# A fused convolution and mixture-of-experts kernel: TensorE multiplies the identity before its first tile, and the first tile's Toeplitz columns come in three parts instead of two

## The reference

```python
x = x + tanh(g_xattn[0]) * xattn(ctx, ctx, layernorm(x), ssm_kernel, D, 8)
x = x + tanh(g_ffn[0]) * ffn(layernorm(x), gate_w, w1, w2, w3, sw1, sw2, sw3)
```

## Time and profile before

| | |
|---|---|
| median of 3 runs | 742.96 us |
| lowest, highest | 740.34, 745.32 us |
| profiled execution, span | 739.8 us |
| TensorE, VectorE, ScalarE, GpSimd busy | 717.1, 568.5, 459.4, 363.4 us |
| TensorE in the first 11.3 us | 0.65 us busy |
| TensorE, 14.5 to 17.4 us | 2.85 us busy |

### The profile page before, as it was taken

How to read it: one execution, slowest core, us unless ns; L and a number is a source line. 1 busy time by engine, 2 the same in 40 slices (tenths; PEclk the granted TensorE clock), 3 DMA queues, 4 the chain that set the end, 5 groups by cost and what they waited for, 6 DMA issues and landing times.

```text
span 739.8 us, 15553 instructions
## 1 busy us (share of the span) xinstructions
PE 717.1 (97%) x4602; PEld 676.3 (91%) x4602; DVE 568.5 (77%) x1111; ACT 459.4 (62%) x659; POOL 363.4 (49%) x190
## 2 busy tenths in 40 slices
PE   3999999999999999999999999999999999999998
PEld 3999999999998999899989999988989999999997
DVE  7899999999965578428899588848987699679942
ACT  6575757575432222126878588847885789578931
POOL 4999888887401065042435433543634354434320
PEclk9999999999999999999999999999999999999999
DMA  6678687877522122463667577766565764432101
GB/s 231 215 239 288 218 272 216 279 218 253 186 85 60 29 43 29 144 197 90 161 201 218 131 232 210 198 176 168 145 182 160 176 193 90 74 68 46 30 1 57
DMA packets 48404, 114.88 MB, mean 155 GB/s; under 512 B 7472, under 2 KB 8624, under 8 KB 48336
## 3 DMA queue, kind: packets, MB, share of 16 engines
q1 hardware_dynamic: 35792, 89.67, 37.1%
q0 software_dynamic: 12544, 24.40, 17.9%
HBM read 157.78 MB, written 29.26 MB: 253 GB/s over the span
## 4 chain that ended last, share of the span: by engine, by line
PE 69%; DVE 13%; DMA 6%; issue 5%; ACT 3%; SPq 1%; ACTq 1%; POOL 1%; DVEq 1%; POOLq 0%
PE pair L1303 19%; PE bank L1303 15%; PE pair L1328 12%; PE pair L1234 8%; PE bank L1328 6%; PE bank L1185 4%; PE pair L1311 3%; DMA out<-ys,slot_info 3%; DMA raw<-in_weights 2%; PE bank L1245 2%; DVE prod L829 2%; DVE bank L834 2%; DVE x L800 2%; DVE w_lo L1150 1%; DVE rows L841 1%
## 5 line engine op out<-in xcount | busy, mean ns | idle before, releaser
L1150 DVE TENSOR_TENSOR w_lo<-raw,w_hi 128x1408 fp32r<-128x1408 f32 x94 | 148.5, 1621 | 47.0 <-ACT w_hi L733 47.0
L1441 POOL DMA_INDIRECT out<-ys,slot_info x47 | 80.6, 1714 | 120.6 <-ACT ys L721 87.3
L1428 POOL DMA_INDIRECT tn<-t_rows,slot_info x47 | 75.5, 1605 | 123.1 <-DVE tT_lo L888 90.6
L733 ACT ACTIVATE w_hi<-raw 128x1408 fp32r x94 | 124.6, 1374 | 2.1 <-issue 1.4
L1234 PE MATMUL pair<-kv_hi,toep_hi 128*128 128x288 f32 x320 | 100.6, 314 | 1.7 <-DMA toep_lo<-kpad_lo 1.4
L1234 PE MATMUL pair<-kv_lo,toep_hi 128*128 128x288 f32 x320 | 95.3, 298 | 0.0
L1234 PE MATMUL pair<-kv_hi,toep_lo 128*128 128x288 f32 x320 | 95.1, 297 | 0.0
L1155 DVE TENSOR_TENSOR w_lo<-raw,w_hi 128x1536 fp32r<-128x1536 f32 x47 | 82.3, 1752 | 4.5 <-ACT w_hi L740 4.5
L1379 POOL TENSOR_TENSOR kv_lo<-kv,kv_hi 128x2304 fp32r<-128x2304 f32 x15 | 77.3, 5153 | 5.9 <-ACT kv_hi L625 5.9
L740 ACT ACTIVATE w_hi<-raw 128x1536 fp32r x47 | 69.3, 1474 | 0.1
L829 DVE TENSOR_TENSOR prod<-pair,q 128x256 f32<-128x256 f32 x128 | 53.4, 417 | 15.1 <-PE pair L1234 9.6
(11 more groups left out here) (223 smaller groups left out, 2009.3 us busy)
## 6 DMA issues: line engine op xcount, KB each, us to landing
raw<-in_weights SPq DMA_DIRECT2D x94, 704.0 KB
raw<-in_weights SPq DMA_DIRECT2D x47, 768.0 KB
toep_hi<-kpad_hi SPq DMA_DIRECT2D x15, 512.0 KB, 4.6
toep_lo<-kpad_lo SPq DMA_DIRECT2D x15, 512.0 KB, 6.2
cx<-in_ctx SPq DMA_DIRECT2D x15, 384.0 KB, 6.3
stage<-in_weights SPq DMA_DIRECT2D x16, 272.0 KB, 6.7
xt<-in_x SPq DMA_DIRECT2D x16, 256.0 KB, 6.4
xr<-in_x SPq DMA_DIRECT2D x16, 256.0 KB, 6.6
```

Of the source, the lines that this page charges most:

```text
L733: act.activation(w_hi[s % 2][:, a:b], raw[:, bass.ds(half + a, b - a)], ACT.Copy).then_inc(hi_ok[n_], 1)
L1150: dve.tensor_tensor(w_lo[s % 2][:, a:b], raw[:, bass.ds(half + a, b - a)], w_hi[s % 2][:, a:b].bitcast(F32), ALU.subtract).then_inc(lo_ok[ ...
L1428: pool.indirect_dma_start(out=tn[o % 3][:], out_offset=None, in_=t_rows, in_offset=bass.IndirectOffsetOnAxis(ap=slot_info[:, 3 * i:3 * i + ...
L1441: pool.indirect_dma_start(out=out, out_offset=bass.IndirectOffsetOnAxis(ap=rows, axis=0), in_=ys[o % 2][:], in_offset=None, bounds_check=R ...
```

## The change

The first tile's Toeplitz columns come as lag 0, lag 1 and lags 2 and 3, with a semaphore each, so SP issues six transfers where it issued four. `conv(0, 1)` waits for the second pair, `conv(0, 2)` for the third. Ahead of the first `turn_q` TensorE waits for square_first and multiplies the identity by itself 12 times into `ps_t`; the result is never read.

```diff
+WARM = 12
...
-        kvh_first, kvl_first, toep_first = sem("kvh_first"), sem("kvl_first"), sem("toep_first")
+        kvh_first, kvl_first = sem("kvh_first"), sem("kvl_first")
+        toep_first, toep_second = sem("toep_first"), sem("toep_second")
...
-            for a, b, landed in ((0, P, toep_first), (P, L, toep_in[0])):
+            for a, b, landed in ((0, P, toep_first), (P, 2 * P, toep_second), (2 * P, L, toep_in[0])):
                 for part, rows in ((toep_hi, toeplitz[0]), (toep_lo, toeplitz[1])):
                     sp.dma_start(part[0][:].bitcast(F32).rearrange("p (h c) -> p h c", h=2)[:, :, a:b],
                                  rows[0][:, :, a:b]).then_inc(landed, 16)
...
                         if t.within(0, 1) and lb == 1:
-                            pe.wait_ge(toep_in[0], 32)
+                            pe.wait_ge(toep_second, 32)
                             pe.wait_ge(kvl_first, 2)
                         if t.within(0, 1) and lb == 2:
+                            pe.wait_ge(toep_in[0], 32)
                             pe.wait_ge(kvl_ok, 1)
...
+            pe.wait_ge(square_first, 1)
+            for _ in range(WARM):
+                pe.matmul(ps_t[:, 0:P], ident[:], ident[:], start=True, stop=True)
             turn_q(At(0))
```

## The result

Over 20 executions each, the changed kernel has a median of 745.73 us (741.13 to 748.06) and the kernel before 743.03 us (740.0 to 745.38). The ratio is 1.0042, 95% interval 1.0027 to 1.0056: 2 to 4 us slower, well inside the 1% that I had called no change, and clear of no change by this larger number of runs. The profiled execution is the fastest of the 20, 741.13 us with a span of 739.3; its span is even 0.5 us shorter than the one shown before. So the trace has to be read by stages, not by its end.

What follows compares the result with a forecast made beforehand. TensorE, busy 717.1 of 739.8 us, bounds the kernel; the edit acts on tile 0's waits. conv(1, 0) at 26.7 (TensorE) against 25.77 adds 1.0, giving 740.8, plus 3.2 for the median: 744.0, range 739.8 to 747.4.

Steps and rivals of the forecast that it cites:

- two terms: At conv(1, 0): GpSimd's line 0.5 us later, to 26.3; TensorE ready at 26.7 after a clock fall; the later counts.
- signs of being wrong: conv(1, 0) before 25.7, forming of tile 2 before 16.4 or after 17.5, or 133 ns matmuls right after the long pause.
- favoured case: Clock falls after tile 0's long pause, TensorE ready for conv(1, 0) at 26.7: +1.0 us, chance 0.45.
- Warm-up: Before turn_q: 24 instructions of 0.20 us end at 10.2, bounds 9.7 to 11.8; costs nothing, faster conv(0, 0) worth nothing.
- The offer: conv(0, 1) starts at 13.2 instead of 14.55, 1.35 us; VectorE's rows until 17.14 leave 0.4 of it.
- The queue: Added issues and 512 packets in SP's queue land cx of tile 2 0.5 us later, bounds 0 and +2.6; conv(1, 0) at 26.3.
- slower by packets: Rival: packets at 141 per us land cx of tile 2 2.6 us late, conv(1, 0) at 28.4, 745.6 us; chance 0.18.
- The clock: After tile 0's 2.4 us pause, 3.4 us at half clock lose 1.7; TensorE starts at 17.2, ready at 26.7.
- The sum: conv(1, 0) at the later of 26.3 and 26.7 against 25.77: +1.0 us, passed unchanged to the end.
- The faster rival: The wait at 25.77 is not GpSimd's, no clock fall, tile 0 keeps its gain: -3.8 us or 739.2; chance 0.10.

Runs made afterwards that it cites:

- bridged: The changed kernel with identity multiplications also filling TensorE's two pauses in tile 0; 743.78 us, ratio 1.0017 to the kernel before.
- warm_only: The kernel before plus only the twelve identity multiplications, with its two-part Toeplitz load kept; 743.65 us, ratio 1.0015.
- change_again: The changed kernel itself, unaltered, run and profiled again in another session beside the kernel before; 744.77 us, ratio 1.0018.
- split_only: The changed kernel without the twelve identity multiplications, so only the three-part Toeplitz load; 744.43 us, ratio 1.0001 to the kernel before.
- cx_early: The changed kernel with x of tile 1 and cx of tile 2 issued before the third Toeplitz part; 743.85 us, ratio 1.0020 to the kernel before.
- cold_again: Third-session repeat of cx_early without the identity multiplications; 741.74 us, ratio 0.9978 to the kernel before.
- cx_early_spun: cx_early plus six identity multiplications in each of TensorE's two tile 0 pauses; 741.91 us, ratio 0.9980 to the kernel before.

## Why the prediction was right

The forecast, 744.0 with no measurable difference and a lean to slower, was right in range, class and sign: 745.73. Its two terms were right in kind; one was mis-sized, and the other was not the one that decides. In size it forecast +1.0 us and +2.5 were measured. One of its own signs of being wrong came true in the profile of the changed kernel: matmuls at 133 ns right after the long pause. So the favoured case, a fall of the clock in tile 0 that makes TensorE late for conv(1, 0), is not what happened, and that the time landed in the range owes something to luck.

- *Warm-up.* 24 instructions, 4.49 us, done at 10.0 (I had 10.2), 0.19 each; 5.45 us in the second profile, between my bounds. Its cost on the path was nothing and what it bought was nothing, as forecast.
- *The offer.* conv(0, 1) at 13.09 against 13.2; VectorE's row ends at 16.94 instead of 17.14, and sum_rows(0, 0) starts at 17.00 instead of 17.58; 0.2 of these 0.6 us are VectorE's, so of 1.35 us some 0.4 remained, then nothing. GpSimd's and VectorE's exclusion, named by the Trainium skill (SBUF - State Buffer, "Who interferes with whom"), stands in both profiles: in the changed kernel VectorE's subtraction of 576 columns takes 0.75 us before GpSimd's forming of 8.85 to 12.33 and about 3.5 us across it (5.39 for two subtractions, less 1.87 for the later one by the earlier trace rows), and this kv_lo of block 1 is what the new wait ends on. That it ends there is not fixed: in bridged, with the same load, conv(0, 1) started at 14.15 and waited for the transfer. This was the sharpest part of the reading: the chain's longest step was worth a third of its length.
- *The queue.* The step that was mis-sized: "I take 0.5". It measures 1.5 us (10.5 against 9.0 us from the first Toeplitz issue), inside my bounds of 0 and +2.6. I had priced the 512 packets at 1.56 us, which is close, and then taken 1.0 us off for the bytes that the old transfer also had to move. That subtraction was the error: in the rows of 9 to 11.5 us both queues move 280 packets per us, and there fewer bytes in each saved nothing. The rate does not stay at 280, so the closeness of 1.56 to 1.5 is partly luck. The rival "slower by packets" named the mechanism and had a price too high. It decides by itself: past +0.9 it passes the clock's term, and it did.
- *The clock.* TensorE was to start at 17.2, lose 1.7 us and be ready at 26.7. In the first profile there was no fall, in the second there was, and neither moved conv(1, 0), since GpSimd was later. The fall and its price are real where nothing hides them (warm_only, +1.2 us), and the changed kernel has about one more slow stretch per execution than before, though not mainly in tile 0. The step failed in its place: not TensorE's line but GpSimd's sets the start.
- *The sum.* The queue's 1.5 us are shown in the traces. The rest, about 1 us of the mean difference of 2.5 +- 1.1 us (20 runs; 2.2 in the other session), goes with the slow stretches, but is not shown to come from them: with the pauses filled the difference is +1.0 +- 1.4. The terms do not add up closely either. The session with change_again has 0.0026 less mean clock than the kernel before it, worth 1.9 us by 740 x 0.0026, and that leaves 0.3 of its 2.2 +- 1.05 us for the queue; part of the slow time must have been hidden, or the error hides the queue's part. Where in the execution the stretches fall that cost time stays open; of two profiles one has its first-tile fall hidden and 6.8 us of half clock at 501 us, the other has none. A fall in the second pause, in front of conv(1, 0), would count in full; it was not caught in a profile.
- *The faster rival* fell: the unnamed releaser at 25.77 is GpSimd's kv_lo, as conv(1, 0) starts 0.10 to 0.11 us after that kv_lo ends in the profiles of before, changed, split_only, change_again and cx_early, wherever cx put it.

## What to carry to other kernels

When the chain of waits names a transfer, look at what every other engine is doing at the moment it lands; the gain ends at the next latest of them, here 0.4 of 1.4 us. Splitting a load also splits its packets and pushes back everything queued behind it, so the question is not only what comes earlier but who is last in that queue and whether someone on the path waits for it; put that one first. A warm-up only helps if the work behind it is dense: full pace in front of waits turns slow work into pauses (2.08 us here), and in two of the five profiles with a warm-up and open pauses the clock fell soon behind one.

## What the runs showed of the hardware that I had not expected

- The granted clock fell to 0.5 after pauses shorter than the 2.3 us I argued from: 2.14 us (warm_only, 15.5 to 22.3 us) and 2.08 us (change_again, 17.7 to 21.0), each with work at full pace between pause and fall. It is a chance, not a certainty: 2.08 us in tile 0 of the changed kernel passed without a fall, and at 501 us it fell after 2.04 us (cold_again) and did not after 3.40 us (cx_early_spun). The pauses of 1.47 and 1.36 us of cx_early had no fall behind them in its profile. The Trainium skill (TensorE: Matmul & The Clock Gate, "HAM oscillation") speaks of waits between bursts of matmuls, longer ones than these; the runs agree in kind.
- The same 280 packets per us carried 138 GB/s in the changed kernel and 236 in the kernel before, when packets of 512 to 1536 B had begun to fill the queue; two microseconds later it was 354 and 159 packets per us at 258 and 232 GB/s. Splitting a transfer into 512 packets more cost what was queued behind it 1.5 us, 3 ns for each, and two more issues cost none.
- The same 24 instructions of identity multiplication lasted 4.49 us in one profile of the changed kernel and 5.45 in the other, 0.19 and 0.23 each. In bridged, at full pace, 18 of them took 2.17 us, 0.12 each.
